# Slot reads and states moved ahead of the v/g tiles, slot scores behind them, in every steady stage

## The reference

```
q, k = rope(xn Wq), rope(xn Wk);  v, g = xn Wv, xn Wg
s  = clip(xn Ws1 Ws2 + b, -32, 32);  es = exp(s);  enz = 1 / cumsum(es)
A  = tril(q k^T) * scale
ok = enz * (A es)              # slot reads: one value per token and slot
qv = softmax(ok);  W2 = tril((qv * enz) es^T)
o  = W2 v;  out += rmsnorm(o) * silu(g) @ Wo
mlp: gelu(xn Wgate) * (xn Wup) @ Wdown
```

## Time and profile before

| | |
|---|---|
| median of 3 runs | 1081.25 us (1080.89 to 1081.56) |
| the profiled execution | 1081.48 us, span 1079.7 us |
| PE busy | 1067.8 us (99%) |
| ACT, POOL busy | 653.8 us (61%), 420.4 us (39%) |
| chain that ended last | PE 93%, DVE 3%, ACT 1%, issue 1%, DMA 1% |
| DMA queues | 6.1% of 16 engines' span |

### The profile page before, as it was taken

One profiled execution on the slowest core, in us unless ns is written; L12 is line 12 of the kernel. 1 busy time (PEld: TensorE's weight loads), 2 busy tenths in 40 slices (PEclk: granted clock), 3 DMA queues, 4 the chain that ended last, 5 costly groups with the idle time before them and its releaser, 6 DMA issues.

```text
span 1079.7 us, 20531 instructions
## 1 busy us (share of the span) xinstructions
PE 1067.8 (99%) x7158; PEld 919.4 (85%) x7158; DVE 916.1 (85%) x1679; ACT 653.8 (61%) x2112; POOL 420.4 (39%) x309
## 2 busy tenths in 40 slices
PE   8999999999999999999999999999999999999999
PEld 6788888888888888888888888888888888888888
DVE  6998888888889888889878898889888889888886
ACT  5766665566655576555766556656565665656564
POOL 5353352434523354232643326343253432524332
PEclk9999999999999999999999999999999999999999
DMA  5020000200002000020000200002000010000001
GB/s 172 1 80 2 1 2 1 81 1 1 2 1 81 1 2 1 2 80 2 1 1 1 80 2 2 1 1 81 1 1 1 9 73 1 1 1 2 20 21 40
DMA packets 9558, 23.06 MB, mean 21 GB/s; under 512 B 880, under 2 KB 5872, under 8 KB 8560
## 3 DMA queue, kind: packets, MB, share of 16 engines
q1 hardware_dynamic: 9456, 21.76, 5.6%
HBM read 19.66 MB, written 2.10 MB: 20 GB/s over the span
## 4 chain that ended last, share of the span: by engine, by line
PE 93%; DVE 3%; ACT 1%; issue 1%; DMA 1%; SPq 0%; POOL 0%; DVEq 0%; POOLq 0%; ACTq 0%
PE bank L221 21%; PE bank L223 21%; PE bank L222 21%; PE bank L326 5%; PE bank L396 5%; PE bank L367 3%; PE bank L339 3%; PE bank L328 3%; PE bank L405 3%; PE bank L316 2%; PE bank L342 1%; PE bank L376 1%; PE bank L389 1%; PE bank L358 1%; PE bank L351 1%
## 5 line engine op out<-in xcount | busy, mean ns | idle before, releaser
L1458 POOL TENSOR_TENSOR inter_lo<-ffb,inter_hi 128x512 fp32r<-128x512 f32 x62 | 79.7, 1309 | 446.5 <-ACT inter_hi L811 446.5
L1449 POOL TENSOR_TENSOR qkT<-ra,xs 128x512 f32<-128x512 f32 x128 | 164.8, 1288 | 136.2 <-DVE xs L1121 114.4
L774 ACT ACTIVATE sm<-bank,mx 128x64 f32<-128x64 f32 x256 | 76.5, 325 | 145.3 <-DVE mx L1077 145.2
L1121 DVE TENSOR_TENSOR xs<-xs,rope 128x512 f32<-128x512 f32 x128 | 130.3, 1018 | 0.0
L755 ACT ACTIVATE xs<-bank 64x512 f32<-64x512 f32 x128 | 76.2, 595 | 79.3 <-PE bank L223 48.4
L1118 DVE TENSOR_TENSOR ra<-bank,rope 128x512 f32<-128x512 f32 x128 | 87.9, 687 | 35.2 <-ACT xs L756 33.4
L1066 DVE RECIPROCAL enzT<-enzT 128x256 f32<-128x256 f32 x64 | 111.6, 1744 | 0.0
L221 PE MATMUL bank<-xh,wgu_hi 128*128 128x512 f32 x256 | 105.3, 411 | 0.0
L221 PE MATMUL bank<-xh,wqk_hi 128*128 128x512 f32 x256 | 103.0, 402 | 0.8 <-DVE ffa L1102 0.8
L221 PE MATMUL bank<-wvg_hi,xh 128*128 128x512 f32 x256 | 100.8, 394 | 1.0 <-DVE xl L1177 1.0
L223 PE MATMUL bank<-xh,wgu_lo 128*128 128x512 f32 x256 | 101.0, 395 | 0.0
(11 more groups left out here) (173 smaller groups left out, 3057.0 us busy)
## 6 DMA issues: line engine op xcount, KB each, us to landing
raw<-in_w_qkvg SPq DMA_DIRECT2D x7, 1024.0 KB, 7.2
scaled<-in_w_scaled SPq DMA_DIRECT2D x8, 640.0 KB, 8.3
packed<-in_w_packed SPq DMA_DIRECT2D x8, 384.0 KB, 3.1
acc<-in_x SPq DMA_DIRECT2D x3, 512.0 KB, 9.6
out<-acc SPq DMA_DIRECT2D x3, 512.0 KB, 3.0
raw<-in_w_qkvg SPq DMA_DIRECT2D x2, 512.0 KB, 6.4
acc<-in_x SPq DMA_DIRECT2D x2, 256.0 KB, 3.0
ws_raw<-in_w_slot SPq DMA_DIRECT2D x8, 48.0 KB, 3.0
```

The source lines that it names most:

```text
L774: ins = act.activation(sm[:, c], src[:, c], ACT.Exp, bias=mx[:, g:g + 1], accum_out=ssum[:, g:g + 1])
L1121: dve.tensor_tensor(two(xs[i % 2][:, :]), two(xs[i % 2][:, :]), sin, ALU.mult).then_inc(sin_done, 1)
L1449: pool.tensor_tensor(qkT[:, i, :], ra[i % 2][:, :], xs[i % 2][:, :], ALU.add).then_inc(roped, 1)
L1458: pool.tensor_tensor(dst[1][e], ffb[e][:, :], dst[0][e].bitcast(F32), ALU.subtract).then_inc(inter_lo, 1)
```

## The change

On TensorE slot_reads and slot_states follow the gated transposes directly, and slot_reads writes to sc[0]; slot_scores comes behind the second v/g tile and waits for okz_done, since sc[0] must have been read. The waits for ogT ahead of the reads and for okz_done in the second outputs are gone. On ScalarE copy_state comes first and slot_exp behind the two copy_v. On VectorE softmax_in takes the place of clip, clip comes after hidden, and the two gate_g stand ahead of cumulate; in stage 1 the reciprocal of the second batch moves ahead of softmax_in.

```diff
@@ TensorE @@
-            def outputs(done, b, hp, free_okz):
+            def outputs(done, b, hp):
...
-                elif free_okz is not None:
-                    pe.wait_ge(okz_done, free_okz)
...
                 gated_transpose(st)
                 pe.wait_ge(A_off, 4 * st + 3)
-                slot_scores(st, nbp, nhp)
+                slot_reads(st, sc[0])
+                slot_states(st, bp)
                 project_vg(st + 1, nbp, nhp, 0, True)
                 project_vg(st + 1, nbp, nhp, 1, True)
-                pe.wait_ge(ogT_hi, 2 * st - 1)
-                pe.wait_ge(ogT_lo, 2 * st - 1)
-                slot_reads(st, rg[0])
-                slot_states(st, bp)
-                outputs(st, 0, php, None)
+                pe.wait_ge(okz_done, st + 1)
+                slot_scores(st, nbp, nhp)
+                outputs(st, 0, php)
                 project_vg(st + 1, nbp, nhp, 2, True)
...
                 slot_rows(st)
-                outputs(st, 1, php, st + 1)
+                outputs(st, 1, php)
@@ ScalarE @@
-                slot_exp(st + 1, npar)
+                copy_state(st)
                 copy_v(st + 1, npar, 0)
                 copy_v(st + 1, npar, 1)
-                copy_state(st)
+                slot_exp(st + 1, npar)
@@ VectorE @@
                 gated_lo(st, 0)
-                clip(st + 1, npar, sc[0][:, :])
+                if st == 1:
+                    invert(st, par, 1)
+                softmax_in(st, par, sc[0])
                 gated_lo(st, 1)
                 gate_gelu(st, 1)
                 hidden(st, 1)
                 if st == 1:
-                    invert(st, par, 1)
                     x_bias(prep)
+                clip(st + 1, npar, sc[0][:, :])
                 gate_g(st + 1, npar, 0)
+                gate_g(st + 1, npar, 1)
                 cumulate(st + 1, npar)
-                gate_g(st + 1, npar, 1)
-                softmax_in(st, par, rg[0])
```

## The result

| | before | changed |
|---|---|---|
| median, 4 runs each | 1081.07 us | 1091.48 us (1091.1 to 1091.79) |
| ratio | | 1.0098 [1.0085, 1.011] |
| span of the profiled execution | 1079.7 us | 1089.3 us |

The forecast was 1091.0 us. TensorE does the same work and waits a little in each stage. Its list of waits, with nothing that recurs in the steady stages before, now has two groups on the slot reads, and VectorE has one on clip. The columns are: who waited for whom, us in total, times, longest.

What follows compares the result with a forecast made beforehand. The prediction took TensorE to bound the kernel. Losses of 8.9 us at the slot reads and 0.9 in stage 1, 9.8 together, on the profiled 1081.48 gave 1091.3 us, 1091.0 as the median; range 1086 to 1097.

Steps and rivals of the forecast that it cites:

- The bound: TensorE is the path, so a reordering pays only if it shortens TensorE's own stream; a stage lasts 32.81 us.
- Part 1: Slot reads directly behind the transposes wait for ScalarE's fourth score copy: 0.17 to 0.70 us a stage, together 8.9 us.
- Part 2: A v/g tile instead of outputs behind the narrow matmuls: difference 0, bounds 6.3 us saved and 3 lost.
- Part 3: Slot scores behind the second v/g tile, now waiting for okz: cost 0, the wait covered by 2.4 us.
- Part 4: VectorE and ScalarE, late slot scores through clip to softmax: cost 0; with bp = 2 0.6 us later, slack 0.69.
- Part 5: First steady stage, reciprocal ahead of softmax_in: slot scores lose 0.8 us, outputs another 0.4; net loss 0.9 us.
- (a): Gaps of the narrow matmuls shrink and the hand-over costs 0.05 us: 1082.8 us, within no change; chance 0.07.
- (b): Faster: the whole 0.30 us of narrow-matmul entry and exit goes in all 30 stages: 1072 us; chance 0.03.
- (c): Slower still: chain of clip, exponential, scan, reciprocal is longer than summed, p_ready late: 1094 or 1110 us; chance 0.09.
- (d): New waits on TensorE bring the clock down; halved in the seven bp = 1 stages, 1320 us; chance 0.01.

Runs made afterwards that it cites:

- mended kernels: The changed kernel with VectorE's fourth score block earlier and stage 1 in the old order, 1082.01 us; also without the reads' wait for the third copy, 1081.46 us.

## Why the prediction was right

- **The bound.** Right: TensorE's starts set everything; 8.98 us in stages 2 to 30, forecast 8.9.
- **Part 1, the copy.** Right in place; the close sum is in part luck. Forecast losses 0.17, 0.70, 0.18, 0.20 for bp = 0 to 3; stage lengths measured 32.97 to 32.99, 33.49, 32.95, 33.03 against 32.80, so 0.18, 0.69, 0.15, 0.23. But the stages grew by more than the copy explains. By their starts the reads are 0.13, 0.65, 0.14 and 0.18 later than t + 0.96 for bp = 0 to 3, 7.8 us in all and not 8.9: the hand-over is 0.10 where I took 0.12 between 0.05 and 0.14, and the copies end up to 0.03 earlier. The other 1.2 us had no term in the forecast, and the two errors nearly cancel; about 1 us of it is still there in the mended kernels (below). The rule that the prediction takes from the Trainium skill, Perfetto Trace Analysis, section Identifying Dependency Chains, is borne out: the trace has the separate semaphore instruction in front of the reads' load, and where the load keeps the copy's wait itself the hand-over is 0.05 against 0.10. All three of these waits are for ScalarE, so several semaphores of one engine are enough for it here.
- **Part 2, neighbours.** Right: in stage 13 the first v/g matmul starts 1.89 after the reads and the second 0.33 after it, as the earlier trace rows had it:

```profile
471.59 0.65 PE L339 MATMUL bank<-At,esJ 128*64 128x256 f32 x4 [0.57 <-ACT At L776]
...
473.48 0.50 PE L221 MATMUL bank<-wvg_hi,xh 128*128 128x512 f32 x1
473.81 0.39 PE L222 MATMUL bank<-wvg_lo,xh 128*128 128x512 f32 x1
```

- **Part 3, slot scores.** Right: no wait for okz in a steady stage, one in stage 1.
- **Part 4, VectorE.** Right, and as thin as said. VectorE in stage 14 answers to the earlier trace rows:

```profile
509.75 0.69 DVE L1042 TENSOR_SCALAR esT<-bank 128x512 f32<-128x512 f32 x1 [0.95 <-PE bank L311]
510.36 0.74 DVE L1048 SCALAR_TENSOR_TENSOR G<-th,bank 128x256 f32<-128x256 f32 x2
511.14 1.28 DVE L1057 TENSOR_TENSOR_SCAN enzT<-esT 128x256 f32<-128x256 f32 x2
512.33 1.73 DVE L1063 RECIPROCAL enzT<-enzT 128x256 f32<-128x256 f32 x1
...
514.50 0.56 DVE L1135 TENSOR_SCALAR codes<-codes 128x768 int32<-128x768 int32 x1
514.98 0.68 DVE L1074 TENSOR_REDUCE mx<-bank 128x8 f32<-128x512 f32 x1
```

  softmax_max starts at t + 11.49 (514.98 - 503.49), forecast t + 11.5, with no wait for L351, and in the other stages it still waits for it, by 0.3 (23 times in the list). The exponentials end at 518.18 and L358 starts at 518.42, as if nothing had happened.
- **Part 5, stage 1.** Right in kind, a third too small: 0.9 forecast, 1.3 measured (38.36 against 37.07). TensorE waits 0.67 us there for okz:

```profile
74.18 0.49 PE L311 MATMUL bank<-h,ws 96*128 96x512 f32 x1 [0.67 <-DVE okz L1069]
...
79.50 0.72 PE L493 MATMUL bank<-ident,xb 128*128 128x128 f32 x4 [0.21 <-ACT xb L819]
```

  The slot scores start at t + 6.54 where t + 5.71 was possible, 0.83 late (0.8 forecast), and the outputs 0.41 more (0.4); they start at t + 7.18 where it was t + 6.06. Another 0.2 us has no term in the forecast: the transposes of x (L493) wait for ScalarE's xb. ScalarE makes xb behind slot_exp, which waits for the moved clip; xb starts at t + 9.64 (77.29) where it was t + 8.31, and ends 0.14 before L493 starts.

- **Rivals.** (a) and (b) need the gaps of the narrow matmuls to shrink. With everything mended the reads still start at t + 0.96 and the time is 1081.46 us, not less. (c) is real with bp = 2 but 0.1 us away; two experiments set it off. (d) fell: the granted clock is 1.00 in the whole window of the changed kernel.

What stays open: stages of the mended kernels last 32.83 us against 32.80, about 1 us in all. It lies in the q/k tiles: slot_softmax starts at t + 14.81 in both kernels, slot_weights behind them at t + 20.83 against t + 20.80. What makes them longer is not known.

## What to carry to other kernels

When a group of matmuls moves forward on the bounding engine, write down for each operand when its producer ends, relative to an anchor that doesn't move, and compare: 0.1 us short of ready costs 0.1 us in every turn of the loop, and the work that ran in between was the cover, not filling. If a step needs to stand there, move its producer first; one step on an engine that is 85% busy took back 8.1 of 10.4 us. Count how often the array changes its shape: here a new order with as many visits to the narrow shape took TensorE as long as the old one, and one visit more cost 0.40 us a stage.

## What the hardware showed that I had not expected

A second visit to the 64-column shape costs 0.40 us a stage, not the 0.30 that the gaps around the first one show. And which of several waits stands first, and so is kept by the weight load itself, is worth 0.05 us a stage, 1.4 us over the 29 stages.
